# Merging the rows of one token over all four experts of a batch, so that both adding scatters write to the output itself

## The chip, the cores and the metric

The kernel runs on one core of a Trainium2 chip. The metric is the device time of one execution in microseconds (us), as the median over several runs; lower is better. The engines are named as in the profile: PE is TensorE's matmul and PEld its weight load, DVE is VectorE, ACT is ScalarE, POOL is GpSimd, SP is SyncE, which here only issues transfers.

## The reference, cut to what matters

Two layers work on x of shape (64, 64, 256), that is T = 4096 tokens of 256 numbers: an attention, a feed-forward over kept tokens, a second attention, and a mixture of experts. Only the last is touched by the change:

```python
logits = x @ gate_w.T                       # 64 experts
probs = softmax(logits); w, sel = top_k(probs, 8); w = w / sum(w)
# each expert takes its first CAP = 64 tokens; a token has up to 8 experts
h = silu(inp @ wg[e]) * (inp @ wu[e])       # (64, 96) per expert
out = h @ wd[e]                             # (64, 256) per expert
y = zeros((T, 256)).at[tok].add(g)          # g: out's rows times w
x = x + y
```

So each of 64 experts yields 64 rows, and each row is added to the row of its token. One token can occur in several experts, thus up to 8 rows are added to the same row of the output.

## The kernel before, in words

The first stages (two attentions, feed-forward, routing) keep the tokens in SBUF, write the residual to the DRAM array `out`, and write the normalised rows with their expert shares to the DRAM array `table`. `fill_slots` (lines 1254 to 1321) finds for each of the 4096 expert slots the token that sits in it; `k.token` is a 128 x 32 array of token numbers, one column for a *pair* of experts (64 slots each, 128 partitions). An empty slot gets the number T + partition, a spare row behind the tokens (L1296 to L1300). `k.move` (L1303) is the distance from a slot's token to its spare row.

`experts` (lines 1325 to 1502) works in 16 batches of four experts, that is two pairs, p = 0 and 1. Each engine has its own instruction stream, and semaphores couple them. For batch n:

- POOL gathers the 2 x 128 rows from `table` with two indirect transfers (L1361), five batches ahead of use. In the loop it first issues the two adding scatters of batch n (L1378), then the two gathers of batch n + 5. There are none left to issue from batch 11 on.
- PE turns the gathered rows (L1400), spreads the token numbers over a row (L1406), which waits until DVE has made the twins of the batch before (L1404), multiplies by the down weights of batch n - 1 (L1415) and by the gate and up weights of batch n (L1426), merges batch n - 1 (L1435) and turns the hidden values (L1442).
- ACT copies the turned rows (L1452), takes the silu (L1456), copies the merged sums of batch n - 1 into `add` (L1463) and then the turned hidden values (L1468). `add` has two places, so L1463 of batch m waits until both scatters of batch m - 2 have landed (L1461, L1462). ACT works in order: what stands behind that wait waits too, and so do PE and DVE.
- DVE copies the down result (L1478), makes the hidden values (L1486), and for each pair a 128 x 128 *twin* matrix that is 1 where two slots hold the same token (L1494). L1494 also counts these per row. L1497 to L1501 then send the second copy of a token to its spare row instead.
- SP loads the weights of batch n + 9 as soon as batch n has used its own (ring of 9 places, seven such loads of 768 + 384 KB in this stage).

The merge and the redirection hold within one pair alone: twin times part gives each slot the sum over both slots of the pair that have its token. Between the two pairs of a batch the same token can still occur, and two adding transfers in flight must not touch the same row. So pair 0 is added to `out` and pair 1 to a second array `extra`, which SP has filled with zeros long before (L1584, L1586), and each scatter waits only for the scatter of the batch before to its own array:

```python
for p, sum_of, landed in ((0, out, e_added), (1, extra, e_extra)):
    if n:
        pool.wait_ge(landed, 16 * n)
    pool.indirect_dma_start(out=sum_of[:, :], ..., compute_op=ALU.add).then_inc(landed, 16)
```

At the end POOL waits for the last scatters, and four transfers of 1 MB each add `extra` to `out` (L1387, the "joining transfers"). After them the program only clears semaphores and passes a barrier.

Of the kernel before, what the change touches and what calls it, by code (L numbers as in the profile page):

```python
# [12 lines left out]
P = 128  # L13
B, S, D = 64, 64, 256
C = 128
T = B * S
# [1237 lines left out]
def fill_slots(nc, ins, k, bank, stack):  # L1254
# [29 lines left out]
    def vector(dve):  # L1284
        dve.wait_ge(k.r_found, NT // GT)
        first_of(dve, k.found[:, :], best, s_max, s_rep)
        dve.wait_ge(s_backc, 1)
        first_of(dve, both[:, :], first[:, 0, :], s_max2, s_rep2)
        dve.wait_ge(s_max2, rounds)
        dve.tensor_copy(first[:, 1, :], first[:, 0, :]).then_inc(s_dup, 1)  # L1290
        dve.wait_ge(s_last, 1)
        for h in range(2):
            rows = slice(64 * h, 64 * h + 64)
            dve.tensor_copy(value[rows, :], bank(2)[rows, 0:E].rearrange("p (j e) -> p j e", e=2)[:, :, h]).then_inc(s_value_s, 1)
        dve.wait_ge(s_value_s, 2)
        dve.tensor_scalar(empty[:, :], value[:, :], 0.0, k.row_number[:, 0:1], ALU.is_equal, ALU.mult).then_inc(s_empty_s, 1)  # L1296
# [6 lines left out]
        dve.tensor_scalar(k.move[:, :], k.token[:, :], -1.0, k.spare_row[:, 0:1], ALU.mult, ALU.add).then_inc(s_move, 1)  # L1303
        dve.wait_ge(s_move, 1)
# [20 lines left out]
def experts(nc, ins, k, bank, out, extra, table):  # L1325

    with ExitStack() as stack:
# [5 lines left out]
        twin = z.sb("e_twin", [P, 2, 2, P])  # L1333
        count, again = z.sb("e_count", [P, 2, 2]), z.sb("e_again", [P, 2, 2])
# [6 lines left out]
        (e_idx_s, e_got0, e_got1, e_got2, e_got3, e_got4, e_got5, e_gotT, e_gotTc, e_row, e_twin_s, e_again_s, e_shift_s, e_to_s,  # L1341
         e_gu, e_silu, e_hid_s, e_hidT, e_hidTc, e_y, e_part_s, e_sum, e_add_s, e_added, e_extra, e_joined
         ) = z.sems(
             "e_idx_s e_got0 e_got1 e_got2 e_got3 e_got4 e_got5 e_gotT e_gotTc e_row e_twin_s e_again_s e_shift_s e_to_s "
             "e_gu e_silu e_hid_s e_hidT e_hidTc e_y e_part_s e_sum e_add_s e_added e_extra e_joined")
# [10 lines left out]
        def gpsimd(pool):  # L1356
            def gather(n, p):
                if n >= GOT_E:
                    pool.wait_ge(e_gotT, n - GOT_E + 1)
                    pool.wait_ge(e_hid_s, 4 * (n - GOT_E + 1))  # L1360
                pool.indirect_dma_start(out=got[:, n % GOT_E, p, :], out_offset=None, in_=table[:, :],  # L1361
                                        in_offset=bass.IndirectOffsetOnAxis(ap=idx[:, 2 * n + p:2 * n + p + 1], axis=0)
                                        ).then_inc(got_in[n % GOT_E], 16)

            pool.wait_ge(k.rows_set, 32 * (NT // GT))
            pool.wait_ge(k.pads, 16 * (3 + NT // 4))
            pool.wait_ge(k.out_set, 16 * NT)
            pool.wait_ge(e_idx_s, 1)
            for n in range(GOT_E - 1):
                for p in range(2):  # L1370
                    gather(n, p)
            for n in range(NB_E):
                pool.wait_ge(e_to_s, n + 1)
                pool.wait_ge(e_add_s, n + 1)
                for p, sum_of, landed in ((0, out, e_added), (1, extra, e_extra)):
                    if n:
                        pool.wait_ge(landed, 16 * n)
                    pool.indirect_dma_start(out=sum_of[:, :], out_offset=bass.IndirectOffsetOnAxis(ap=to[:, n, p:p + 1], axis=0),  # L1378
                                            in_=add[:, n % 2, p, :], in_offset=None, compute_op=ALU.add).then_inc(landed, 16)
                for p in range(2):  # L1380
                    if n + GOT_E - 1 < NB_E:
                        gather(n + GOT_E - 1, p)
            pool.wait_ge(e_added, 16 * NB_E)
            pool.wait_ge(e_extra, 16 * NB_E)
            for c in range(4):
                rows = slice(c * T // 4, (c + 1) * T // 4)
                pool.dma_start(out=out[rows, :].rearrange("(a b) d -> a (b d)", b=4), in_=extra[rows, :].rearrange("(a b) d -> a (b d)", b=4),  # L1387
                               accum_op=ALU.add, max_dma_last_dim=8192).then_inc(e_joined, 16)
            pool.wait_ge(e_joined, 64)

        def tensor(pe):
            for n in range(NB_E + 1):
                v, w, m = n % 2, (n - 1) % 2, n - 1
                if n < NB_E:
# [8 lines left out]
                    if n:  # L1403
                        pe.wait_ge(e_twin_s, 2 * n)  # L1404
# [24 lines left out]
                if n:  # L1429
                    pe.wait_ge(e_part_s, n)  # L1430
                    pe.wait_ge(e_twin_s, 2 * n)
# [13 lines left out]
        def scalar(act):  # L1445
            for n in range(NB_E + 1):
# [23 lines left out]
        def vector(dve):  # L1470
            dve.tensor_copy(idx[:, :], k.token[:, :]).then_inc(e_idx_s, 1)  # L1471
            for n in range(NB_E + 1):
# [6 lines left out]
                if n < NB_E:  # L1479
# [31 lines left out]
def program(nc, ins, out, extra, table):  # L1511
    with ExitStack() as stack:
# [22 lines left out]
        k.row_number, k.spare_row, k.second = z.sb("row_number", [P, 1]), z.sb("spare_row", [P, 1]), z.sb("second", [P, 1])  # L1535
# [207 lines left out]
        x = experts(nc, ins, k, bank, out, extra, table)  # L1743
# [27 lines left out]
def shape_constants():  # L1771
# [12 lines left out]
        "row_number": p[:, None].astype(np.float32),  # L1784
        "spare_row": (T + p)[:, None].astype(np.float32),
# [57 lines left out]
```

## Time and profile before

| what | value |
|---|---|
| median of 3 runs | 1038.46 us (1035.84 to 1041.59) |
| the profiled execution, its own time | 1038.37 us |
| its span in the profile | 1036.6 us |
| mean granted clock of TensorE | 0.938 |
| PE busy in the span | 853.5 us (82%) |
| DVE / ACT / POOL busy | 663.1 / 425.1 / 338.0 us |
| the stage with the experts | from about 888 us to the end |

The span counts from the first to the last instruction of the profiled execution; its own time is 1.8 us longer and lies within 0.1 us of the median. A row of a timeline is: start, duration, engine, line, operation, output from input, and in brackets how long the engine had stood idle before it and what ended that. The time of an indirect transfer on POOL is the time in which POOL writes its descriptors, not that in which data moves; its landing is seen by what waits for it. A row of busy times by stretches gives, for a stretch, its length, the busy time of PE, PEld, DVE, ACT and POOL with their counts, the granted clock of PE, the mean busy share of the 16 DMA engines, and GB/s.

### The profile page before, as it was taken

The numbers are of one execution on the slowest core, as the hardware profiler recorded it, in microseconds if no ns is written. First come the engines' busy times: TensorE is split into PE (matmuls) and PEld (weight loads), VectorE is DVE, ScalarE is ACT, GpSimd is POOL, SyncE is SP. The second block draws the span as 40 slices with busy tenths as digits, with TensorE's granted clock in tenths as the row PEclk, the third lists the DMA queues.
The fourth block names the chain that finished last, engine by engine and source line by source line (L and its number), as shares of the span: only waits on it lengthen the run. The fifth ranks groups of instructions, "written<-read, shape, count | busy, mean of one in ns | idle before, by whom it ended". The sixth has DMA issues, their size and how long they took to land. (4 is left out here: it accounts for less than half of the span.)

```text
span 1036.6 us, 25512 instructions
## 1 busy us (share of the span) xinstructions
PE 853.5 (82%) x9176; PEld 659.7 (64%) x9176; DVE 663.1 (64%) x1469; ACT 425.1 (41%) x1011; POOL 338.0 (33%) x297
## 2 busy tenths in 40 slices
PE   1799999999999899999889999999998830468730
PEld 0577777777777689899667777777776720245520
DVE  5577777777777665555367777777775589344520
ACT  1243443444444433334365555566656730123210
POOL 1443343443433040000133333333332010367860
PEclk9899999999999999999999999999999875698985
DMA  9300000000005000000011111111110494397557
GB/s 297 84 14 14 15 10 15 15 10 15 15 10 185 4 12 0 0 0 0 3 18 25 30 30 30 30 30 30 30 33 22 139 347 133 93 272 180 92 62 151
DMA packets 79561, 64.78 MB, mean 62 GB/s; under 512 B 41120, under 2 KB 74144, under 8 KB 79008
## 3 DMA queue, kind: packets, MB, share of 16 engines
q1 hardware_dynamic: 72800, 50.62, 16.7%
q0 software_dynamic: 6720, 13.64, 7.1%
q8 instruction: 24, 0.39, 0.2%
q14 instruction: 17, 0.14, 0.0%
HBM read 45.97 MB, written 22.45 MB: 66 GB/s over the span
## 5 line engine op out<-in xcount | busy, mean ns | idle before, releaser
L402 ACT ACTIVATE pr_t<-bank 128x512 f32<-128x512 f32 x128 | 76.4, 597 | 160.8 <-PE bank L298 160.0
L822 POOL TENSOR_TENSOR g_k_bd<-g_k_t,head_mask 128x1024 f32<-128x1024 f32 x32 | 60.6, 1893 | 134.8 <-ACT g_k_t L997 134.8
L310 PEld LDWEIGHTS bank<-v_bd,pr_t 128*64 128x64 f32 x2048 | 70.0, 137 | 26.6 <-issue 26.4
L298 PE MATMUL bank<-ident,sub 128*128 128x128 f32 x512 | 82.5, 284 | 3.6 <-ACT pr_t L402 2.8
L310 PE MATMUL bank<-v_bd,pr_t 128*64 128x18 f32 x2048 | 82.8, 214 | 0.1
L298 PEld LDWEIGHTS bank<-ident,sub 128*128 128x128 f32 x512 | 56.1, 141 | 31.4 <-issue 17.6
L479 DVE TENSOR_TENSOR sub<-bank,top 128x2048 f32<-128x2048 f32 x32 | 73.3, 2292 | 3.9
L259 POOL TENSOR_TENSOR rot<-part_a,part_b 128x512 f32<-128x512 f32 x32 | 40.7, 1273 | 103.8 <-DVE part_b L488 103.8
L475 DVE TENSOR_REDUCE top<-bank 128x32 f32<-128x2048 f32 x32 | 73.1, 2285 | 0.6 <-PE bank L286 0.4
L817 POOL TENSOR_TENSOR xres<-xres,g_out_bias 128x256 f32 (+1 forms) x32 | 23.3, 728 | 152.5 <-DVE g_xn L1020 152.5
L646 ACT ACTIVATE f_hid<-bank,b 128x128 f32<-128x128 f32 x128 | 36.5, 368 | 85.6 <-PE bank L592 85.6
L267 POOL TENSOR_TENSOR k_bd<-qk_t,head_mask 128x1024 f32<-128x1024 f32 x32 | 60.6, 1893 | 31.2 <-ACT qk_t L417 31.2
L592 PE MATMUL bank<-f_xs_t,w 128*128 128x128 f32 x512 | 63.8, 278 | 0.0
L592 PEld LDWEIGHTS bank<-f_xs_t,w 128*128 128x128 f32 x512 | 59.6, 192 | 5.0 <-ACT f_hid L646 4.6
L630 PE MATMUL bank<-w,f_hid 128*128 128x256 f32 x256 | 57.9, 379 | 0.0
L954 ACT ACTIVATE g_sq<-g_qk 128x512 f32<-128x512 f32 x32 | 20.2, 630 | 81.8 <-DVE g_qk L1070 81.8
L630 PEld LDWEIGHTS bank<-w,f_hid 128*128 128x128 f32 x256 | 47.4, 190 | 5.8
L1361 POOL DMA_INDIRECT e_got<-table,e_idx x32 | 31.8, 994 | 55.9 <-DVE e_idx L1471 46.4
L488 DVE TENSOR_TENSOR part_a<-bank,cos_t 128x512 f32<-128x512 f32 x32 | 22.2, 692 | 38.2 <-PE bank L359 38.2
L262 POOL TENSOR_TENSOR xres<-xres,bo 128x256 f32 (+1 forms) x32 | 23.3, 729 | 69.9 <-DVE xn L470 69.9
L875 PEld LDWEIGHTS bank<-g_v_bd,g_pr_t 128*64 128x64 f32 x1024 | 35.3, 136 | 15.7 <-issue 15.7
L964 ACT ACTIVATE g_pr_t<-bank 128x512 f32<-128x512 f32 x64 | 38.2, 597 | 16.7 <-PE bank L861 15.9
(196 smaller groups left out, 2008.8 us busy)
## 6 DMA issues: line engine op xcount, KB each, us to landing
e_w_gu<-in_experts_in SPq DMA_DIRECT2D x16, 768.0 KB, 14.0
e_w_d<-in_experts_out SPq DMA_DIRECT2D x16, 384.0 KB, 17.0
table<-r_row SPq DMA_DIRECT2D x16, 320.0 KB, 8.4
xres<-in_x SPq DMA_DIRECT2D x4, 1024.0 KB, 9.4
extra<-zero SPq DMA_DIRECT2D x8, 512.0 KB, 5.8
out<-xres SPq DMA_DIRECT2D x32, 128.0 KB, 1.7
out<-extra POOLq DMA_DIRECT2D x4, 1024.0 KB, 14.1
keys_in<-in_ctx_t SPq DMA_DIRECT2D x32, 64.0 KB, 1.8
```

Of the source, the lines that this page charges most:

```text
L259: pool.tensor_tensor(rot[:, v, :], part_a[:, v, :], part_b[:, v, :], ALU.add).then_inc(a_rot, 1)
L267: pool.tensor_tensor(k_bd[:, v, :, :, :, :].rearrange("p c b h s -> p (c b) h s"), qk_t[:, v, KC:2 * KC, :].rearrange("p c (b a s) -> p (c ...
L298: m = pe.transpose(b_pr[:, j * P:(j + 1) * P], sub[:, v, cols], k.ident[:, :])
L310: m = pe.matmul(b_o[64 * b:64 * b + 64, hp * VW0:(hp + 1) * VW0], pr_t[:, e, j, b * S:(b + 1) * S], v_bd[:, v, b, hp, :], start=True, stop ...
L402: act.activation(pr_t[:, e, :, :].rearrange("p j q -> p (j q)"), b_pr[:, :], ACT.Exp).then_inc(a_exp, 1)
L475: dve.tensor_reduce(top[:, :], sc, AX.X, ALU.max).then_inc(a_top, 1)
L479: dve.tensor_tensor(sub[:, u, :].rearrange("p (h s) -> p h s", s=S), sc, stretch(top[:, :], S), ALU.subtract).then_inc(a_sub, 1)
L592: mm = pe.matmul(b_h[half][:, (c % 4) * P:(c % 4 + 1) * P], k.w1[:, d, c * P:(c + 1) * P], xs_t[:, u, d, :], start=(d == 0), stop=(d == KC ...
L630: mm = pe.matmul(b_y[:, 0:D], hid[:, u, c, :], k.w2[:, c, :], start=(c == 0), stop=(c == FC - 1))
L646: act.activation(hid[:, u, c, :], b_h[c // 4][:, (c % 4) * P:(c % 4 + 1) * P], ACT.Gelu_apprx_tanh, bias=k.b1[:, c:c + 1]).then_inc(f_gelu, 1)
L822: pool.tensor_tensor(k_bd[:, v, :, :, :, :].rearrange("p c b h s -> p (c b) h s"), k_t[:, v, :, :].rearrange("p c (b a s) -> p (c b) a s", ...
L964: act.activation(pr_t[:, e, :, :].rearrange("p j q -> p (j q)"), b_pr[:, :], ACT.Exp).then_inc(g_exp, 1)
```

## The change

The twins are now made between all four experts of a batch: two pairs times two pairs, four 128 x 128 matrices instead of two. The merging matmul sums over both pairs, so each slot gets the sum over the whole batch. The first occurrence in the batch keeps its token's row, every other goes to a spare row; with two pairs there are 2 x 128 spare rows. All rows that the two scatters of a batch touch then differ, and both go to `out`. Both scatters of a batch wait until both of the batch before have landed. `extra`, its zero fill and the joining transfers are gone.

```diff
-            pool.wait_ge(k.pads, 16 * (3 + NT // 4))
+            pool.wait_ge(k.pads, 16 * 4)
...
-                for p, sum_of, landed in ((0, out, e_added), (1, extra, e_extra)):
-                    if n:
-                        pool.wait_ge(landed, 16 * n)
-                    pool.indirect_dma_start(out=sum_of[:, :], out_offset=bass.IndirectOffsetOnAxis(ap=to[:, n, p:p + 1], axis=0),
-                                            in_=add[:, n % 2, p, :], in_offset=None, compute_op=ALU.add).then_inc(landed, 16)
+                if n:
+                    pool.wait_ge(e_added, 32 * n)
+                for p in range(2):
+                    pool.indirect_dma_start(out=out[:, :], out_offset=bass.IndirectOffsetOnAxis(ap=to[:, n, p:p + 1], axis=0),
+                                            in_=add[:, n % 2, p, :], in_offset=None, compute_op=ALU.add).then_inc(e_added, 16)
...
-            pool.wait_ge(e_added, 16 * NB_E)
-            pool.wait_ge(e_extra, 16 * NB_E)
-            for c in range(4):
-                rows = slice(c * T // 4, (c + 1) * T // 4)
-                pool.dma_start(out=out[rows, :].rearrange("(a b) d -> a (b d)", b=4), in_=extra[rows, :].rearrange("(a b) d -> a (b d)", b=4),
-                               accum_op=ALU.add, max_dma_last_dim=8192).then_inc(e_joined, 16)
-            pool.wait_ge(e_joined, 64)
+            pool.wait_ge(e_added, 32 * NB_E)
...
                     if n:
-                        pe.wait_ge(e_twin_s, 2 * n)
+                        pe.wait_ge(e_twin_s, 4 * n)
...
                     for p in range(2):
-                        mm = pe.matmul(b_sum[:, p * D:(p + 1) * D], twin[:, w, p, :], part[:, w, p, :], start=True, stop=True)
+                        for q in range(2):
+                            mm = pe.matmul(b_sum[:, p * D:(p + 1) * D], twin[:, w, q, p, :], part[:, w, q, :],
+                                           start=(q == 0), stop=(q == 1))
...
                     if n >= 3:
-                        act.wait_ge(e_added, 16 * (n - 2))
-                        act.wait_ge(e_extra, 16 * (n - 2))
+                        act.wait_ge(e_added, 32 * (n - 2))
...
+                    for q in range(2):
+                        for p in range(2):
+                            dve.tensor_scalar(twin[:, v, q, p, :], b_row[:, p * P:(p + 1) * P], k.token[:, 2 * n + q:2 * n + q + 1],
+                                              None, ALU.is_equal, ALU.add, accum_out=count[:, v, q, p:p + 1]).then_inc(e_twin_s, 1)
+                    dve.wait_ge(e_twin_s, 4 * (n + 1))
                     for p in range(2):
-                        dve.tensor_scalar(twin[:, v, p, :], b_row[:, p * P:(p + 1) * P], k.token[:, 2 * n + p:2 * n + p + 1],
-                                          None, ALU.is_equal, ALU.add, accum_out=count[:, v, p:p + 1]).then_inc(e_twin_s, 1)
-                    dve.wait_ge(e_twin_s, 2 * (n + 1))
-                    dve.tensor_scalar(again[:, v, :], count[:, v, :], -1.0, k.second[:, 0:1], ALU.add, ALU.mult).then_inc(e_again_s, 1)
-                    dve.wait_ge(e_again_s, n + 1)
+                        dve.tensor_scalar(front[:, v, p:p + 1], count[:, v, p, p:p + 1], -1.0, k.second[:, 0:1],
+                                          ALU.add, ALU.mult).then_inc(e_front_s, 1)
+                    dve.wait_ge(e_front_s, 2 * (n + 1))
+                    dve.tensor_copy(again[:, v, 0:1], front[:, v, 0:1]).then_inc(e_again_s, 1)
+                    dve.tensor_scalar(again[:, v, 1:2], front[:, v, 1:2], count[:, v, 1, 0:1], 0.5, ALU.add, ALU.is_gt).then_inc(e_again_s, 1)
+                    dve.wait_ge(e_again_s, 2 * (n + 1))
...
-            sp.dma_start(out[T:T + P, :], k.zero[:, 0:D]).then_inc(k.pads, 16)
-            sp.dma_start(table[T:T + P, :], k.zero[:, :]).then_inc(k.pads, 16)
-            for c in range(NT // 4):
-                sp.dma_start(extra[4 * P * c:4 * P * (c + 1), :].rearrange("(t p) d -> p t d", p=P),
-                             spread(k.zero[:, 0:D], 4)).then_inc(k.pads, 16)
-            sp.dma_start(extra[T:T + P, :], k.zero[:, 0:D]).then_inc(k.pads, 16)
+            for h in range(2):
+                sp.dma_start(out[T + h * P:T + (h + 1) * P, :], k.zero[:, 0:D]).then_inc(k.pads, 16)
+                sp.dma_start(table[T + h * P:T + (h + 1) * P, :], k.zero[:, :]).then_inc(k.pads, 16)
```

In `fill_slots` the constants `row_number` and `spare_row` become 128 x 32 arrays, with 128 more in the columns of pair 1, and L1296 and L1303 become `scalar_tensor_tensor` with them as second input.

## Rows read from the trace of the kernel before

**Rows 1.** The chain of waits, 996 to 1037 us: start, duration, what.
```profile
996.61 3.75 DMA out<-e_add,e_to
...
1003.00 3.80 DMA extra<-e_add,e_to
```

**Rows 2.** The joining transfers' line L1387: issue and landing.
```profile
L1387 POOL DMA_DIRECT2D out<-extra x4: 934/1307/1766, 1007.4 to 1009.1; - x4
...
DMA to landing us min/median/max: 7.6/14.1/20.6
```

**Rows 3.** Busy time by stretches, the end of the span.
```profile
1010.00:1028.00 18.00, 0.00 (x0) 0.00 (x0) 0.00 (x0) 0.00 (x0) 0.86 (x2) 0.50 1.04 215
```

**Rows 4.** Timeline of POOL, batches without gathers.
```profile
987.43 1.55 POOL L1378 DMA_INDIRECT out<-e_add,e_to  x1 [1.25 <-DMA out<-e_add,e_to]
989.28 1.55 POOL L1378 DMA_INDIRECT extra<-e_add,e_to  x1 [0.30 <-issue]
...
1001.14 1.55 POOL L1378 DMA_INDIRECT out<-e_add,e_to  x1 [1.12 <-DMA out<-e_add,e_to]
```

**Rows 5.** Timeline of POOL, a batch with gathers after the weight loads.
```profile
957.03 1.61 POOL L1378 DMA_INDIRECT out<-e_add,e_to  x1 [0.30 <-issue]
958.95 1.57 POOL L1378 DMA_INDIRECT extra<-e_add,e_to  x1 [0.30 <-issue]
...
963.44 1.62 POOL L1378 DMA_INDIRECT out<-e_add,e_to  x1 [0.30 <-DVE e_to L1501]
...
982.69 1.61 POOL L1378 DMA_INDIRECT out<-e_add,e_to  x1 [0.30 <-issue]
```

**Rows 6.** Timeline of POOL, batches beside the weight loads.
```profile
907.01 1.64 POOL L1378 DMA_INDIRECT out<-e_add,e_to  x1 [5.05 <-DVE e_to L1501]
...
914.21 1.62 POOL L1378 DMA_INDIRECT out<-e_add,e_to  x1 [1.06 <-issue]
...
922.16 1.62 POOL L1378 DMA_INDIRECT out<-e_add,e_to  x1 [1.84 <-DMA out<-e_add,e_to]
...
932.85 1.58 POOL L1378 DMA_INDIRECT extra<-e_add,e_to  x1 [2.66 <-DMA extra<-e_add,e_to]
...
943.78 1.61 POOL L1378 DMA_INDIRECT out<-e_add,e_to  x1 [0.30 <-issue]
```

**Rows 7.** Timeline of ACT: copies into add that waited for a landing.
```profile
922.13 0.60 ACT L1463 ACTIVATE e_add<-bank 128x512 f32<-128x512 f32 x1 [2.26 <-DMA extra<-e_add,e_to]
...
950.49 0.60 ACT L1463 ACTIVATE e_add<-bank 128x512 f32<-128x512 f32 x1 [0.55 <-DMA extra<-e_add,e_to]
...
962.87 0.60 ACT L1463 ACTIVATE e_add<-bank 128x512 f32<-128x512 f32 x1 [2.47 <-DMA extra<-e_add,e_to]
```

**Rows 8.** Busy time by stretches, with and without weight loads.
```profile
904.00:950.00 46.00, 35.26 (x256) 24.07 (x256) 22.71 (x86) 12.77 (x29) 31.21 (x24) 0.89 0.93 254
952.00:980.00 28.00, 23.03 (x176) 15.81 (x175) 13.86 (x53) 8.27 (x19) 22.59 (x18) 0.94 0.56 90
```

**Rows 9.** Timeline, all engines: an unblocked batch, and the clock's low stretch.
```profile
954.72 1.13 PE L1435 MATMUL bank<-e_part,e_twin 128*128 128x256 f32 x4
954.84 0.33 ACT L1456 ACTIVATE e_act_g<-bank 128x192 f32<-128x192 f32 x1 [1.97 <-PE bank L1426]
...
956.58 0.35 DVE L1494 TENSOR_SCALAR_CACHE_REDUCE e_twin<-bank,token 128x128 f32<-128x128 f32 x1
...
956.61 0.42 PE L1442 MATMUL bank<-ident,e_hid 128*96 128x128 f32 x2 [0.75 <-DVE e_hid L1486]
...
957.13 0.09 DVE L1494 DVE_READ_ACCUMULATOR e_twin<-bank,token 128x1 f32 x1
...
960.07 0.33 ACT L1456 ACTIVATE e_act_g<-bank 128x192 f32<-128x192 f32 x1 [1.97 <-PE bank L1426]
...
974.29 0.33 ACT L1456 ACTIVATE e_act_g<-bank 128x192 f32<-128x192 f32 x1 [3.68 <-PE bank L1426]
```

**Rows 10.** Transfers issued by SP: the zero fill of extra.
```profile
323.19 9.03 SPq L1584 DMA_DIRECT2D extra<-zero  x8
```

More of the change, by code:

```diff
@@ L1295, in vector @@
         dve.wait_ge(s_value_s, 2)
-        dve.tensor_scalar(empty[:, :], value[:, :], 0.0, k.row_number[:, 0:1], ALU.is_equal, ALU.mult).then_inc(s_empty_s, 1)
+        dve.scalar_tensor_tensor(out=empty[:, :], in0=value[:, :], scalar=0.0, in1=k.row_number[:, :],
+                                 op0=ALU.is_equal, op1=ALU.mult).then_inc(s_empty_s, 1)
         dve.tensor_scalar(name[:, :], value[:, :], -1.0, float(T), ALU.mult, ALU.add).then_inc(s_name_s, 1)
@@ L1301, in vector @@
         dve.wait_ge(s_token, 1)
-        dve.tensor_scalar(k.move[:, :], k.token[:, :], -1.0, k.spare_row[:, 0:1], ALU.mult, ALU.add).then_inc(s_move, 1)
+        dve.scalar_tensor_tensor(out=k.move[:, :], in0=k.token[:, :], scalar=-1.0, in1=k.spare_row[:, :],
+                                 op0=ALU.mult, op1=ALU.add).then_inc(s_move, 1)
         dve.wait_ge(s_move, 1)
@@ L1321, in fill_slots, with experts @@
     return Stage(z.signals, sync=sync, tensor=tensor, scalar=scalar, vector=vector)
-def experts(nc, ins, k, bank, out, extra, table):
+def experts(nc, ins, k, bank, out, table):
     with ExitStack() as stack:
@@ L1332, in experts @@
         got_t = z.sb("e_got_t", [P, 2, 2, KC, P])
-        twin = z.sb("e_twin", [P, 2, 2, P])
-        count, again = z.sb("e_count", [P, 2, 2]), z.sb("e_again", [P, 2, 2])
+        twin = z.sb("e_twin", [P, 2, 2, 2, P])
+        count, front = z.sb("e_count", [P, 2, 2, 2]), z.sb("e_front", [P, 2, 2])
+        again = z.sb("e_again", [P, 2, 2])
         shift = z.sb("e_shift", [P, 2, 2])
@@ L1340, in experts @@
         add = z.sb("e_add", [P, 2, 2, D])
-        (e_idx_s, e_got0, e_got1, e_got2, e_got3, e_got4, e_got5, e_gotT, e_gotTc, e_row, e_twin_s, e_again_s, e_shift_s, e_to_s,
-         e_gu, e_silu, e_hid_s, e_hidT, e_hidTc, e_y, e_part_s, e_sum, e_add_s, e_added, e_extra, e_joined
+        (e_idx_s, e_got0, e_got1, e_got2, e_got3, e_got4, e_got5, e_gotT, e_gotTc, e_row, e_twin_s, e_front_s, e_again_s, e_shift_s, e_to_s,
+         e_gu, e_silu, e_hid_s, e_hidT, e_hidTc, e_y, e_part_s, e_sum, e_add_s, e_added
          ) = z.sems(
-             "e_idx_s e_got0 e_got1 e_got2 e_got3 e_got4 e_got5 e_gotT e_gotTc e_row e_twin_s e_again_s e_shift_s e_to_s "
-             "e_gu e_silu e_hid_s e_hidT e_hidTc e_y e_part_s e_sum e_add_s e_added e_extra e_joined")
+             "e_idx_s e_got0 e_got1 e_got2 e_got3 e_got4 e_got5 e_gotT e_gotTc e_row e_twin_s e_front_s e_again_s e_shift_s e_to_s "
+             "e_gu e_silu e_hid_s e_hidT e_hidTc e_y e_part_s e_sum e_add_s e_added")
         got_in = [e_got0, e_got1, e_got2, e_got3, e_got4, e_got5]
@@ L1430, in tensor @@
                     pe.wait_ge(e_part_s, n)
-                    pe.wait_ge(e_twin_s, 2 * n)
+                    pe.wait_ge(e_twin_s, 4 * n)
                     if n >= 2:
@@ L1508, in over_rows, with program @@
     return vector.rearrange("(a d) -> a d", a=1).to_broadcast([rows, vector.shape[0]])
-def program(nc, ins, out, extra, table):
+def program(nc, ins, out, table):
     with ExitStack() as stack:
@@ L1534, in program @@
         k.countdown = z.sb("countdown", [P, NT])
-        k.row_number, k.spare_row, k.second = z.sb("row_number", [P, 1]), z.sb("spare_row", [P, 1]), z.sb("second", [P, 1])
+        k.row_number, k.spare_row, k.second = z.sb("row_number", [P, NP_E]), z.sb("spare_row", [P, NP_E]), z.sb("second", [P, 1])
         k.token, k.move, k.idx = z.sb("token", [P, NP_E]), z.sb("move", [P, NP_E]), z.sb("e_idx", [P, NP_E], U32)
@@ L1741, in program @@
         nc.all_engine_barrier()
-        x = experts(nc, ins, k, bank, out, extra, table)
+        x = experts(nc, ins, k, bank, out, table)
         inner = stack.enter_context(ExitStack())
@@ L1783, in shape_constants @@
         "countdown": (T - P * np.arange(NT).reshape(2, NT // 2).T.reshape(1, NT) - p[:, None]).astype(np.float32),
-        "row_number": p[:, None].astype(np.float32),
-        "spare_row": (T + p)[:, None].astype(np.float32),
+        "row_number": (p[:, None] + P * (np.arange(NP_E) % 2)).astype(np.float32),
+        "spare_row": (T + p[:, None] + P * (np.arange(NP_E) % 2)).astype(np.float32),
         "second": (p >= CAP)[:, None].astype(np.float32),
@@ L1835 @@
            for n, v in laid.items()}
-    out = nc.dram_tensor("out", [T + P, D], F32, kind="ExternalOutput").ap()
-    extra = nc.dram_tensor("extra", [T + P, D], F32, kind="Internal").ap()
-    table = nc.dram_tensor("table", [T + P, ROW], F32, kind="Internal").ap()
-    program(nc, ins, out, extra, table)
+    out = nc.dram_tensor("out", [T + 2 * P, D], F32, kind="ExternalOutput").ap()
+    table = nc.dram_tensor("table", [T + 2 * P, ROW], F32, kind="Internal").ap()
+    program(nc, ins, out, table)
     r = run_bass_kernel_spmd(nc, [arrays], core_ids=[0])
```

## The prediction

> **What bounds the kernel now.** I read the chain of waits at the end of the span first, because the change removes the last thing in it. The last scatter to `extra` starts at 1003.00 us and lands 3.80 us later, at 1006.80; only then does POOL issue the four joining transfers [rows 1]. They are issued from 1007.4 to 1009.1, and the longest landing takes 20.6 us, so the last one lands at 1029.7 [rows 2]. For 18 us of that the 16 DMA engines are full (share 1.04) at 215 GB/s, and every compute engine stands still [rows 3]. That is 22.9 us, from 1006.8 to 1029.7, with nothing beside them.
>
> Then I read POOL's timeline in the stage of the experts, to see what sets the pace of the 16 batches. There are three regimes, and the reader should see that the change meets each differently.
>
> - Batches 11 to 15 have no gathers left. A first scatter starts 4.6 us after the one before, when that one has landed: from 982.69 to 1001.14, four periods take 18.45 us [rows 4, 5].
> - Batches 7 to 10 are full of POOL's own work: two scatters and two gathers follow each other with gaps of 0.30 us, and the period is 6.41 us (957.03 to 963.44) [rows 5].
> - Batches 0 to 6 run while SP's seven weight loads fill the DMA engines: share 0.93 against 0.56 later [rows 8]. Landings are late, and the seven periods from 907.01 to 957.03 take 50.0 us, 7.15 each [rows 5, 6].
>
> PE, DVE and ACT are not the limit there. Where nothing blocks them a batch takes 5.23 us, from the silu at 954.84 to that at 960.07 [rows 9], and they wait at the copy into `add` for scatters to land [rows 7].
>
> **The change part by part.** The sum is made against the profiled execution, 1038.4 us, which is the median of the runs shown within 0.1 us.
>
> *Joining transfers gone: -22.9 us.* Worked out above. Behind the last landing the program ends as before. The last batch needs both scatters landed, which it needed before too.
>
> The Trainium skill, "DMA: Bandwidth & Descriptors", section "Anatomy of one DMA — SWDGE (gpsimd) path", fits a transfer issued by GpSimd as 2.0 us plus bytes over 436 GB/s. By it 4.2 MB would be an estimated 11.6 us, half of what the rows show, and the change would lose about 2 us instead of gaining. The trace does not agree: 18 us and more of full DMA engines, presumably because an adding transfer also reads what it adds to. The rows leave that course no chance, and the sum goes by them.
>
> *Tail, four periods: +7.3 us.* A first scatter now waits for both scatters of the batch before. The second starts 1.85 us after the first (987.43 and 989.28 [rows 4]), lands 3.80 later [rows 1], and POOL starts 0.78 after a landing it waited for (a scatter of 996.61 lands 3.75 later, at 1000.36, and the next starts at 1001.14 [rows 1, 4]). A period is 1.85 + 3.80 + 0.78 = 6.43, and 6.50 where gathers still made the first longer (1.61 in place of 1.55). Together 25.8 against 18.45.
>
> *Batches 7 to 10: +0.4 us.* Here the wait is nearly hidden by the two gathers: the second scatter starts at 1.92, lands at 5.72, POOL is ready to start at 6.50, against 6.41 now. So 4 x 0.1. If the lag is part of the 0.30 gap, nothing.
>
> *Batches 0 to 6: +4.4 us, the term that I know least.* In the present landings a period would be: batch 1, second landing just before 922.13, so 922.0 - 914.21 + 0.78 = 8.6 (ACT starts 0.1 behind a landing, as 962.87 is against 958.95 + 3.80); batch 2, 932.85 - 922.16 = 10.7; batch 5, 950.4 - 943.78 + 0.78 = 7.4 [rows 5 to 7]. With 8.6 for batch 0, 7.4 for 3 and 4 as for 5, and 6.5 for batch 6, the seven give 56.6, that is +6.6. The lower bound is 0: the loads' bytes are fixed, and with more time between them landings come sooner; the wait only adds, so I exclude a gain. Between them I go by the DMA share. At 0.93 the loss would be 6.6, at 0.56 it is 7 x 0.1 = 0.7. The 46 us at 0.93 are 42.8 us of full DMA engines; spread over 50 us that is a share of 0.86, over 54 us 0.79 [rows 8]. I take 0.79, an estimate, since the loads follow compute, which now waits too, and interpolate: 0.7 + 5.9 x 0.23/0.37 = 4.4 (at 0.86 it would be 5.5).
>
> The same page, section "Latency and other measured facts", says that HBM access takes longer under load and the fixed cost of a transfer is smaller with less. If that were all, the loss would sit near 0.7 and the sum near 1025.4.
>
> *More twins, more merging: +1.5 us once, else hidden.* DVE makes two more twins per batch. Two take 0.64 from the first's start to the last read of its count (956.58 to 957.22), so two more are 0.6. PE's L1406 of the next batch waits for them, and behind it stand L1415 and L1426 of PE and then silu: the unblocked batch becomes 5.8. PE merges with eight passes in place of four, +1.0 (four take 1.13); it waited 0.75 before L1442 anyway, so this stays under the twins [rows 9]. DVE's small steps (two fronts, a copy and a compare in place of one operation) cost at most as much again as two twins, 0.6, an estimate, and end before the copy of the down result is due; the scatter's indices are a batch ahead. 5.8 is below 6.4, so POOL covers all this; without that cover it is 0.6 per batch. Only batch 0 has none: its scatter waits for twins (+0.6) and merge (+0.95), so it starts 1.5 late. Bounds 0.6 to 2.
>
> *At nothing:* the zero fill and its nine issues (8 take 9.03 us of SP [rows 10]; no engine waited for them, and SP's next loads came later); the larger constants and pads, for the same reason; two DVE operations of 128 x 32 with another form, at most 0.1.
>
> **The sum.** -22.9 + 7.3 + 0.4 + 4.4 + 1.5 = -9.3: **1029.1 us**. The range of this case: 1024.7 (nothing lost in batches 0 to 6) to 1031.8 (6.6 lost, batch 0 late by 2).
>
> **The rivals.**
>
> *Contention feeds itself, 1036 us.* With both scatters due before either of the next, a late landing stops POOL, then ACT at `add`, then PE, DVE and the loads behind them, which then bunch. If five of the seven periods took 9.65, the mean of those worked out for batches 1 and 2, and two 6.5, they make 61.3, a loss of 11.3 in place of 4.4: 1036.0. For it: share 0.93, and batch 2 [rows 6, 8]. Against: the loads are only seven, and slower compute spaces them.
>
> *Compute becomes the bound, 1037 us.* The granted clock has a mean of 0.94 from 952 to 980, which is 3.4 us at the lower of its two levels, 1.2 GHz [rows 8]. The silu of 974.29 waited 3.68 for PE in place of 1.97: +1.7 [rows 9]. An unblocked batch at that level is 5.8 + 1.7, and 1.0 more for the longer merge, 8.5 against POOL's 6.5. If four more batches fell there, 4 x 2.0 = 8. For it: PE's waits become longer. Against: PE also gets more work, and `add` is one batch ahead.
>
> *Two adding scatters into one array hinder each other: slower, up to 1065 us.* No row shows this; before, the two in flight had different arrays. Place: the landing of each second scatter. Price: of 3.80 us, 2.25 lie behind the 1.55 in which POOL writes descriptors; served one after the other, 16 x 2.25 = 36 [rows 1, 4]. From 0.6 us per batch on the gain is gone (9.3/16), from 0.9 on it is slower than can be told from no change. Against: the rows that they touch differ.
>
> *The joining was worth less than it shows* (it does not do what it says): only if something else held the end; after 1006.8 nothing else runs [rows 3]. I give it nothing.
>
> **How the numbers follow.** A measurement of this kernel can tell about 0.5%, 5.2 us, from no change. Forecast 0.66; nothing lost beside the loads, at the low end near 1024.7, 0.10; contention 0.12; compute 0.06; hindering scatters 0.06. The first two are faster by over 5.2 us almost always, contention half of the time: 0.82. Within: the other half, compute, and a part of the forecast's edge: 0.12. Slower: 0.06. The range 1024.5 to 1034.0 takes in the forecast's bounds and the nearer half of contention.
>
> **What would show it.** No DMA-bound stretch at the end, and about 7 us from the last landing to the end. First scatters 6.4 to 6.5 apart from batch 7 to 15, now alike with and without gathers. Batch 0's first scatter at 908.5, batch 7's near 962.9, batch 15's near 1014.7 in place of 1001.14, which is also 908.5 + 54.4 + 4 x 6.5 + 25.8. Wrong would be: a second scatter landing later than 3.8 us after its start where no loads run (the third rival), ACT's silu periods above 6.5 with PE at the lower clock (the second), batch 7 behind 966 (the first).

## The result and the profile after

The changed kernel takes 1035.05 us (median of 20 runs), against 1038.43 for the kernel before (also 20); the ratio is 0.9964, with a 95% interval of 0.9947 to 0.9982. It is faster by 3.7 us (1.9 to 5.5), which is within the 0.5% that the prediction called no change. The forecast was 1029.1 us, 9.3 less, with a range of 1024.5 to 1034.0; the measured time lies above that range. The profiled execution took 1035.25 us with a span of 1033.4.

The joining transfers are gone, but most of their 22.9 us has come back as waits between scatters. POOL's timeline of the changed kernel shows where (start, duration, operation, idle time before it):

```profile
889.70 1.21 POOL L1364 DMA_INDIRECT e_got<-table,e_idx  x1 [46.34 <-DVE e_idx L1469]
...
909.59 1.63 POOL L1381 DMA_INDIRECT out<-e_add,e_to  x1 [7.40 <-ACT e_add L1461]
...
918.53 1.62 POOL L1381 DMA_INDIRECT out<-e_add,e_to  x1 [2.82 <-DMA out<-e_add,e_to]
...
926.12 1.62 POOL L1381 DMA_INDIRECT out<-e_add,e_to  x1 [1.48 <-ACT e_add L1461]
...
937.25 1.62 POOL L1381 DMA_INDIRECT out<-e_add,e_to  x1 [5.02 <-ACT e_add L1461]
939.17 1.58 POOL L1381 DMA_INDIRECT out<-e_add,e_to  x1 [0.30 <-issue]
...
946.91 1.62 POOL L1381 DMA_INDIRECT out<-e_add,e_to  x1 [3.55 <-ACT e_add L1461]
...
956.08 1.62 POOL L1381 DMA_INDIRECT out<-e_add,e_to  x1 [3.06 <-ACT e_add L1461]
...
969.29 1.62 POOL L1381 DMA_INDIRECT out<-e_add,e_to  x1 [0.50 <-ACT e_add L1461]
...
995.40 1.62 POOL L1381 DMA_INDIRECT out<-e_add,e_to  x1 [0.41 <-issue]
...
1021.29 1.56 POOL L1381 DMA_INDIRECT out<-e_add,e_to  x1 [2.90 <-DMA out<-e_add,e_to]
1023.15 1.56 POOL L1381 DMA_INDIRECT out<-e_add,e_to  x1 [0.30 <-issue]
```

Read the first scatters of the batches against [rows 4 to 6]. Batch 0 starts at 909.59, batch 7 at 969.29, batch 11 at 995.40, batch 15 at 1021.29. Batch 7 behind 966 was the prediction's sign for its rival "contention feeds itself". From these the whole difference of the spans (3.2 us) can be laid out:

| stretch, us | before | after | difference | forecast |
|---|---|---|---|---|
| start to first gather | 889.45 | 889.70 | +0.3 | 0 |
| first gather to batch 0 | 17.56 | 19.89 | +2.3 | +1.5 |
| batches 0 to 7, seven periods | 50.02 | 59.70 | **+9.7** | **+4.4** |
| batches 7 to 11 | 25.66 | 26.11 | +0.4 | +0.4 |
| batches 11 to 15 | 18.45 | 25.89 | +7.4 | +7.3 |
| batch 15 to the end | 35.46 | 12.11 | -23.3 | -22.9 |

Five of the six are within 1 us of the forecast. The miss is the stretch beside the weight loads, where the seven periods are 8.94, 7.59, 11.13, 9.66, 9.17, 6.58 and 6.63 us (batches 0 to 6).

The chain of waits of the changed kernel (start, duration, what) shows what the periods of batches 2 and 3 are made of:

```profile
928.05 8.38 DMA out<-e_add,e_to
936.43 0.02 issue
936.45 0.02 ACTq L1460
936.47 0.04 issue
936.51 0.61 ACT e_add L1461
937.12 0.13 issue
937.25 0.30 POOL out L1381
...
939.17 6.92 DMA out<-e_add,e_to
```

The second scatter of batch 2 starts at 928.05 and lands 8.38 us later, at 936.43. That one landing releases two engines: ACT, whose copy for batch 4 starts at 936.51, and POOL, whose scatter of batch 3 starts at 937.25. (The release of POOL is put down to ACT's copy, though POOL's scatter is of batch 3, whose copy ended at 926.05; 937.25 is 0.82 after the landing, the usual lag behind a landing.) ACT's release lets PE go on, and PE's matmuls let SP load the next weights. SP's timeline:

```profile
939.49 0.33 SPq L1247 DMA_DIRECT2D e_w_gu<-in_experts_in  x1
939.86 0.43 SPq L1249 DMA_DIRECT2D e_w_d<-in_experts_out  x1
```

So a load of 1.2 MB (768 + 384 KB) is issued 0.3 us after the batch's second scatter, which then lands 6.92 us after its start. PE's clock has a part in this moment: the granted clock had fallen to 0.50 behind PE's wait for ACT, and L1412 took 1.98 us for eight passes instead of 1.08. What that shift by 0.9 us is worth was not tried.

Not every load follows a landing, however. The first five of the seven loads come at PE's own pace; the second to fifth are 5.8 us apart. The last two, at 939.49 above and at 948.26, come later because of the waits:

```profile
910.74 0.33 SPq L1247 DMA_DIRECT2D e_w_gu<-in_experts_in  x1
...
916.52 0.33 SPq L1247 DMA_DIRECT2D e_w_gu<-in_experts_in  x1
...
922.28 0.33 SPq L1247 DMA_DIRECT2D e_w_gu<-in_experts_in  x1
...
928.16 0.33 SPq L1247 DMA_DIRECT2D e_w_gu<-in_experts_in  x1
...
948.26 0.33 SPq L1247 DMA_DIRECT2D e_w_gu<-in_experts_in  x1
```

The load of 928.16 starts 0.1 us after the second scatter of batch 2, the one that took 8.38 us to land. The kernel before has the same meeting, and nearly the same landing (timeline of POOL, then of SP):

```profile
924.08 1.57 POOL L1378 DMA_INDIRECT extra<-e_add,e_to  x1 [0.30 <-issue]
...
924.22 0.33 SPq L1247 DMA_DIRECT2D e_w_gu<-in_experts_in  x1
```

That scatter landed about 8.0 us after its start, since the next one to `extra` began at 932.85 [rows 6], which by the usual lag is 0.78 behind the landing. But the first scatter of the next batch, to `out`, did not wait for it and had begun at 928.57, 6.41 after the one before. With the common wait the period is 11.13. So in batches 0 to 2 landings that were about as late before now cost their full length, and in batches 3 and 4 the loads come, in addition, 2 to 3 us behind the landing that was waited for, that is beside the next second scatter (939.49 and 948.26; second scatters at 939.17 and 948.84).

The busy times by stretches (length, PE, PEld, DVE, ACT, POOL, granted clock, DMA share, GB/s) show, around batch 3, the DMA engines doing almost nothing while everything waits, and then everything at once:

```profile
936.00:938.00 2.00, 0.57 (x4) 0.38 (x6) 0.00 (x0) 1.35 (x3) 0.75 (x1) 0.67 0.05 18
938.00:940.00 2.00, 2.00 (x14) 1.26 (x12) 0.55 (x1) 0.00 (x0) 1.70 (x2) 0.50 0.35 34
940.00:942.00 2.00, 2.00 (x15) 1.12 (x11) 0.15 (x1) 0.00 (x0) 1.70 (x2) 0.50 0.94 172
942.00:944.00 2.00, 2.00 (x6) 1.68 (x7) 1.49 (x5) 0.33 (x1) 1.06 (x2) 0.62 0.95 376
```

### The profile page after: what moved, and what is told of

It reads as the page before. It is cut to its first block and busy times, and to the rows that moved or that the text cites. A ratio compares the mean times of both kernels' runs of the same rounds, so it can differ in the third digit from the quotient of the medians.

```text
span 1033.4 us, 25740 instructions
## 1 busy us (share of the span) xinstructions
PE 870.1 (84%) x9240; PEld 673.2 (65%) x9240; DVE 676.8 (65%) x1581; ACT 424.2 (41%) x1011; POOL 335.0 (32%) x293
## 5 line engine op out<-in xcount | busy, mean ns | idle before, releaser
L310 PEld LDWEIGHTS bank<-v_bd,pr_t 128*64 128x64 f32 x2048 | 70.0, 137 | 26.5 <-issue 26.3
L1381 POOL DMA_INDIRECT out<-e_add,e_to x32 | 50.9, 1590 | 42.9 <-ACT e_add L1461 27.1
L592 PE MATMUL bank<-f_xs_t,w 128*128 128x128 f32 x512 | 63.8, 278 | 0.0
```

Source lines behind the costliest of these rows:

```text
L310: m = pe.matmul(b_o[64 * b:64 * b + 64, hp * VW0:(hp + 1) * VW0], pr_t[:, e, j, b * S:(b + 1) * S], v_bd[:, v, b, hp, :], start=True, stop ...
L592: mm = pe.matmul(b_h[half][:, (c % 4) * P:(c % 4 + 1) * P], k.w1[:, d, c * P:(c + 1) * P], xs_t[:, u, d, :], start=(d == 0), stop=(d == KC ...
L1381: pool.indirect_dma_start(out=out[:, :], out_offset=bass.IndirectOffsetOnAxis(ap=to[:, n, p:p + 1], axis=0), in_=add[:, n % 2, p, :], in_o ...
```

## The experiments

Three theories stood against each other. *Theory 1*: the common wait (no scatter of a batch before both of the last have landed) releases scatters and load in step, and turns every late landing into lost time. These are two claims, and the runs below bear on them differently. *Theory 2*: two adding scatters into one array hinder each other. *Theory 3*: the larger merge slows compute. Profiles of different runs differ by up to 5 us in when the experts' stage begins (first gather from 884.5 to 889.7), so the runs are compared by their periods inside the stage, in us, and by their ratios of times. Ratios are against the kernel before; the reference times of before in these rounds were 1037.0 to 1037.4 us.

| run | median | ratio (95%) | batches 0-7 | 7-11 | 11-15 |
|---|---|---|---|---|---|
| before | 1038.4 | 1 | 50.0 | 25.7 | 18.5 |
| changed | 1035.1 | 0.9964 (0.9947 to 0.9982) | 59.7 | 26.1 | 25.9 |
| no_join | 1012.3 | 0.9762 (0.9723 to 0.9801) | 50.0 | 25.7 | 18.3 |
| pair_wait | 1061.2 | 1.0237 (1.0198 to 1.0276) | 63.8 | 26.2 | 26.3 |
| merge_alone | 1038.8 | 1.0014 (0.9993 to 1.0035) | 50.2 | 25.7 | 18.3 |
| after_no_loads | 1019.6 | 0.9835 (0.9805 to 0.9866) | 46.8 | 26.7 | 25.8 |
| before_no_loads | 1032.5 | 0.9955 (0.9929 to 0.9981) | 45.0 | 25.7 | 18.4 |
| small_runs | 1033.2 | 0.9972 (0.9948 to 0.9997) | 60.4 | 26.3 | 25.9 |
| whole_late | 1028.8 | 0.9909 (0.9869 to 0.9949) | 55.0 | 26.7 | 25.8 |
| thirds_at_once | 1034.9 | 0.9972 (0.9957 to 0.9987) | 57.8 | 26.6 | 25.9 |
| paced_thirds | 1026.0 | 0.9899 (0.9869 to 0.9930) | 47.8 | 26.5 | 28.4 |
| paced_early | 1022.9 | 0.9866 (0.9845 to 0.9886) | 48.4 | 27.0 | 25.5 |
| before_paced | 1033.9 | 0.9965 (0.9949 to 0.9981) | 46.5 | 27.1 | 18.8 |

### The change taken apart: no_join, pair_wait, merge_alone

**no_join.** The kernel before without the joining transfers; half of the sums are missing from its output.

```diff
-            for c in range(4):
-                rows = slice(c * T // 4, (c + 1) * T // 4)
-                pool.dma_start(out=out[rows, :]..., in_=extra[rows, :]..., accum_op=ALU.add, ...).then_inc(e_joined, 16)
-            pool.wait_ge(e_joined, 64)
```

> The kernel before without the four joining transfers; the half of the sums in extra is left out of the output. Both theories (what was lost lies beside the weight loads; or the scatters into one array hinder each other) say the same here: the joining was worth 22.9 us, so the time is about 1015.5 us, and the batches keep their starts (seven periods of 7.15 us, then 6.4, then 4.6).

Measured: 1012.3 us. By the ratio the joining cost 24.7 us (20.6 to 28.7), in agreement with the 22.9 of the trace. The time is 3 us below the 1015.5 expected; the profile's stage of experts starts 3.6 us earlier than before (first gather at 885.88). The largest term of the sum was right.

**pair_wait.** The kernel before, with the common wait alone; arrays, merge and joining stay.

```diff
+                if n:
+                    pool.wait_ge(e_added, 16 * n)
+                    pool.wait_ge(e_extra, 16 * n)
                 for p, sum_of, landed in ((0, out, e_added), (1, extra, e_extra)):
-                    if n:
-                        pool.wait_ge(landed, 16 * n)
```

> The kernel before with one edit: both scatters of a batch wait for both of the batch before; two arrays, the small merge and the joining transfers stay. Theory 1 (the common wait lets weight loads and scatters start together, so that landings stay late): the seven first periods go from 50.0 to 57 to 60 us, the tail's four from 18.4 to 25.9, and the time is 1053 to 1056 us. Theory 2 (two adding scatters into one array hinder each other): here they have two arrays, so the first seven periods take at most 53 us and landings beside the loads are as before; the time is 1046 to 1049 us. Theory 3 (the larger merge slows compute, and that costs the time): as theory 2.

Measured: 1061.2 us, +24.6 us by the ratio (20.5 to 28.6). The wait alone costs what the joining gives. It is above what theory 1 had said (1053 to 1056), and far from theories 2 and 3. Here the scatters go to two arrays and the merge is small, and still the first seven periods take 63.8 us. Its second scatters beside the loads land 6.6 to 8.2 us after their start. The same alternation of empty and full DMA engines stands in its busy times by stretches:

```profile
936.00:938.00 2.00, 1.82 (x10) 1.07 (x12) 0.00 (x0) 0.61 (x2) 1.69 (x2) 0.50 0.03 8
938.00:940.00 2.00, 2.00 (x16) 1.50 (x14) 0.69 (x1) 0.00 (x0) 1.70 (x2) 0.50 1.01 119
...
942.00:944.00 2.00, 1.30 (x9) 0.82 (x8) 1.62 (x9) 0.00 (x0) 0.10 (x1) 1.00 1.04 279
...
946.00:948.00 2.00, 1.77 (x20) 1.38 (x22) 0.64 (x1) 0.67 (x2) 1.66 (x2) 1.00 0.00 0
```

**merge_alone.** The changed kernel given back its two arrays, own waits, zero fill and joining, so that only the merge over four experts is new.

```diff
-                if n:
-                    pool.wait_ge(e_added, 32 * n)
-                for p in range(2):
-                    pool.indirect_dma_start(out=out[:, :], ...).then_inc(e_added, 16)
+                for p, sum_of, landed in ((0, out, e_added), (1, extra, e_extra)):
+                    if n:
+                        pool.wait_ge(landed, 16 * n)
+                    pool.indirect_dma_start(out=sum_of[:, :], ...).then_inc(landed, 16)
...
+            (the four joining transfers and the zero fill of extra, as before)
```

> The changed kernel with two arrays, each scatter waiting for its own array alone, zero fill and joining transfers: against the kernel before only the merge over four experts is new. Theory 1: batch 0 starts 2.3 us late and the seven first periods stay near 50 us, so 1040 to 1042 us. Theory 3 (compute): the seven first periods take 55 us or more, so over 1045 us. Theory 2 says as theory 1.

Measured: 1038.8 us, +1.5 by the ratio, with an interval that includes no change, and a little below the 1040 to 1042 that theory 1 had said. From the first scatter on it keeps the pace of before; the stage begins with the first gather at 885.64:

```profile
905.61 1.64 POOL L1381 DMA_INDIRECT out<-e_add,e_to  x1 [7.45 <-ACT e_add L1468]
...
955.76 1.61 POOL L1381 DMA_INDIRECT out<-e_add,e_to  x1 [0.30 <-issue]
```

The seven periods take 50.15 us; from first gather to batch 0 it is 19.97, as in the changed kernel. Theory 3 falls, and the late start of batch 0 belongs to the merge. The other profiles agree: from first gather to batch 0 the five with the small merge take 16.3 to 18.5 us, the eight with the large one 19.5 to 21.0, by the means 3.1 more.

### The loads: after_no_loads, before_no_loads

Both leave out the seven loads, so batches 9 to 15 multiply by the weights of batches 0 to 6:

```diff
-            for n in range(RING_E, NB_E):
-                sp.wait_ge(e_gu, n - RING_E + 1)
-                sp.wait_ge(e_y, n - RING_E + 1)
-                load_experts(sp, ins, k, n)
...
-                    pe.wait_ge(k.w_in[n % RING_E], 32 * (n // RING_E + 1))
+                    pe.wait_ge(k.w_in[n % RING_E], 32)
```

> The changed kernel without the seven weight loads beside the experts; batches 9 to 15 multiply by the weights of batches 0 to 6, so their output is not the reference's. Theory 1: with no loads each of the first seven periods is 6.4 to 6.6 us, 45.5 in all in place of 59.7, and the time is about 1021 us (14 less than 1035). Theory 2: landings stay late at 8 us or more after the first scatter, the seven take over 55 us, and the time is over 1030 us. Theory 3: between, with ACT's silu periods and not landings setting the pace.

Measured: 1019.6 us, 17.1 less than before by the ratio and so about 13.4 less than the changed kernel. The seven periods fall from 59.7 to 46.8, six of them at 6.5 to 6.6:

```profile
905.46 1.63 POOL L1378 DMA_INDIRECT out<-e_add,e_to  x1 [8.49 <-DVE e_to L1502]
...
952.25 1.62 POOL L1378 DMA_INDIRECT out<-e_add,e_to  x1 [0.47 <-DVE e_to L1502]
```

With both scatters in one array and no loads beside them, the periods are those of a landing in quiet. Theory 2 falls here too.

> The kernel before without the seven weight loads beside the experts (batches 9 to 15 multiply by the weights of batches 0 to 6, so that their output is not the reference's). Theory 1 (the common wait turns what the loads delay into lost time, and two arrays hide most of it): the seven first periods go from 50.0 to 45 us, so 1032 to 1033 us, a third of the 15.4 us that the changed kernel gained by the same edit. If the loads cost both kernels alike, it gains 15 us too, 1022 us, and the common wait is not what makes them dear.

Measured: 1032.5 us, 4.7 less (2.0 to 7.4). The same seven loads cost the kernel before 5 us and the changed one over 13. The loads are the same; the common wait makes them dear. That late landings become lost time is shown by these two runs and pair_wait.

### When and how the loads are issued

**small_runs** was to tell whether the length of the loads' runs matters.

```diff
-                load_experts(sp, ins, k, n)
+                sp.dma_start(k.w_gu[:, n % RING_E, :, :, :].rearrange("p e c i -> p (e c) i"), ...)
+                sp.dma_start(k.w_d[:, n % RING_E, :, :], ...)
```

> The changed kernel with the same loads at the same moments, written as runs of 1536 and 1024 bytes instead of 6144 and 4096. If a scatter's rows of 1 KB are held up because each waits behind one long run of the loads, shorter runs let them land earlier: seven periods of 52 to 56 us in place of 59.7, and 1027 to 1032 us. If it is the loads' bytes alone, or if the shorter runs take longer for the same bytes, the seven take 59 us or more, and 1035 us or more.

Inconclusive: its page counts the same packets as the changed kernel's, so the transfers had stayed the same and the question stays open. As a repeat of the changed kernel it gives the spread: 60.4 against 59.7 us for the seven periods. The line of its page on DMA packets:

```profile
DMA packets 74906, 56.61 MB, mean 55 GB/s; under 512 B 40944, under 2 KB 70000, under 8 KB 74864
```

**whole_late** has the whole loads wait for a landing too, the one that also releases the next first scatter:

```diff
                 sp.wait_ge(e_y, n - RING_E + 1)
+                sp.wait_ge(e_added, 32 * (n - RING_E + 1))
                 load_experts(sp, ins, k, n)
```

> The changed kernel with the whole loads, each released in addition by the landing of the batch's own scatters, that is up to 5 us later or at the moment at which the next scatter is issued. Theory 1, as far as the moment counts: a load of 1.1 MB still takes over 3 us of full engines and reaches into the scatters' data, so the seven periods take 54 to 60 us, and the time is 1030 to 1036 us. If the moment were all, they would take below 52 us, and 1027 us or less.

Measured: 1028.8 us, with 55.0 us for the seven periods, now at 6.6 to 9.6 instead of up to 11.1. The time is below the 1030 to 1036 us expected. Moving the same transfers by some microseconds gives 4.7 us of the periods back; the moment counts, but is not all. It also corrects theory 1: here every load is released by the same landing as a scatter, and yet less is lost. Such a load is issued about 0.7 us ahead of the first scatter of a batch, as in batch 2 (timeline of SP, then of POOL):

```profile
922.96 0.33 SPq L1247 DMA_DIRECT2D e_w_gu<-in_experts_in  x1
...
923.69 1.62 POOL L1382 DMA_INDIRECT out<-e_add,e_to  x1 [3.47 <-ACT e_add L1462]
```

In the changed kernel the loads beside the three longest periods come within 0.6 us of the second scatter. So what hurts is not the shared release itself, but at what moment of the period the load comes, and how much of it.

**thirds_at_once** and **paced_thirds** cut each load in three pieces of 384 KB (two of the gate and up weights, one of the down weights). The first issues all three as the whole load is issued now. The second releases two at each landing up to batch 8, then one. In both, PE waits for all three pieces of a batch before it multiplies by its gate and up weights (80 in place of 64 arrivals; the diffs below leave that line out).

```diff
-                load_experts(sp, ins, k, n)
+                for part in range(3):
+                    load_third(sp, ins, k, n, part)
```

> The changed kernel with each load cut into thirds, all three issued at the moments at which the whole load is issued now. Theory 1 (a load in one piece beside a scatter holds it up, and the thirds help only through their spacing): as the changed kernel, seven first periods of 57 to 61 us and 1033 to 1036 us. If the cutting itself did it, the seven take below 52 us and the time is about 1026 us.

```diff
+            pieces = [(n, part) for n in range(RING_E, NB_E) for part in range(3)]
+            for j in range(1, NB_E - 2):
+                sp.wait_ge(e_added, 32 * j)
+                for n, part in pieces[0:2 if j < 9 else 1]:
+                    sp.wait_ge(e_gu, n - RING_E + 1)
+                    sp.wait_ge(e_y, n - RING_E + 1)
+                    load_third(sp, ins, k, n, part)
+                pieces = pieces[2 if j < 9 else 1:]
```

> The changed kernel with the same loads in thirds of 384 KB, each released by the landing of the scatters of a batch: two at each of batches 1 to 8, one at each of 9 to 13. Theory 1: a third is through before the second scatter's data moves, and landings come near the 5.7 us of the unloaded batches; the first seven periods take 46 to 50 us, later ones stay below 6.8, and the time is 1021 to 1026 us. Rival (what counts is the bytes moved beside the scatters, whenever they are issued): the seven periods take 55 us or more and the time is 1031 to 1037 us.

Measured: cut but not spaced, 57.8 us for the seven and 1034.9 us, the changed kernel within the noise. Cut and spaced, 47.8 us and 1026.0 us. The bytes are the same in both, and cutting alone gives nothing clear; what does it is when the pieces are issued, that is spaced out and at a landing (the two together; whole_late shows the second to be a part of it). The late part of the forecast for paced_thirds failed in one place, the period before batch 14 took 9.02 us. Its timeline, all engines, says why:

```profile
994.50 0.33 SPq L1261 DMA_DIRECT2D e_w_d<-in_experts_out  x1
995.26 1.56 POOL L1398 DMA_INDIRECT out<-e_add,e_to  x1 [3.04 <-DMA out<-e_add,e_to]
...
998.07 2.83 PE L1440 MATMUL bank<-e_w_gu,e_got_t 128*64 128x192 f32 x16 [7.97 <-issue]
...
1004.28 1.56 POOL L1398 DMA_INDIRECT out<-e_add,e_to  x1 [5.59 <-ACT e_add L1478]
```

The last piece was issued at 994.50, and PE, which needs all three, stood 7.97 us, until 3.57 after that issue. **paced_early** issues two pieces at each landing until none is left:

```diff
-            for j in range(1, NB_E - 2):
+            for j in range(1, NB_E - 4):
...
-                for n, part in pieces[0:2 if j < 9 else 1]:
+                for n, part in pieces[0:2]:
```

> The paced thirds with two pieces at each landing until none is left (batches 1 to 11), so that the last piece is in two batches earlier. The period of 9.0 us before batch 14, in which PE waited for weights, should fall to 6.5; the first seven stay as they were. So 2.5 us less than the paced thirds: 1023 to 1024 us. If that period was not due to the last piece, no change.

Measured: 1022.9 us, the long period gone (6.16 us in place of 9.02), the best of all kernels here that leave nothing out: 1.3% faster than before and by the ratios about 10 us faster than the changed kernel. From 910 us to 974 its DMA share is above 0.5 in every stretch of 2 us:

```profile
936.00:938.00 2.00, 1.65 (x12) 0.95 (x13) 1.90 (x13) 1.35 (x3) 1.69 (x2) 1.00 0.78 183
938.00:940.00 2.00, 2.00 (x24) 1.51 (x24) 1.14 (x5) 0.00 (x0) 1.70 (x2) 1.00 1.07 207
940.00:942.00 2.00, 2.00 (x12) 1.44 (x8) 0.93 (x3) 0.33 (x1) 0.42 (x2) 1.00 0.54 150
```

**before_paced** is the kernel before with the same pacing (waits on e_added and e_extra at 16 * j).

> The kernel before with the same pacing of the loads (two thirds at each landing of both scatters). Theory 1: there the loads cost only the 4.8 us by which it is faster without them, so at most that is to be had: 1033 to 1037 us. If pacing gives as much as in the changed kernel (9 us), the loads' cost has nothing to do with the common wait: 1028 us.

Measured: 1033.9 us, 3.6 less than before (2.0 to 5.3), against 10 that the same pacing gave the changed kernel. This is what theory 1 says. Paced alike, the change is worth 10.3 us by the ratios (11.0 by the medians, 1033.9 and 1022.9), more than the 9.3 that were forecast for it.

## Why the prediction was wrong

**Joining transfers, -22.9: right.** 24.7 by no_join, 23.3 in the trace. The estimate from the Trainium skill ("DMA: Bandwidth & Descriptors", "Anatomy of one DMA — SWDGE (gpsimd) path"), 11.6 us for 4.2 MB, was rightly set aside: the trace does not agree with that fit for these adding transfers.

**Tail, +7.3: right** (+7.4). So was the period made of 1.85 + 3.80 + 0.78. **Batches 7 to 10, +0.4: right.**

**Batch 0 late by 1.5: too small**, above its upper bound of 2 too. It was 2.3 in the two profiles, 2.4 with the merge alone, 3.1 by the means of all profiles. In the changed kernel L1423 of batch 1 took 2.72 us for 16 passes, with PE's mean granted clock at 0.75 from 904 to 908; before, the engine was at the full clock at that point. Whether the merge delays the rise of the clock was not tried.

**Batches 0 to 6, +4.4: the step that failed.** It was +9.7, even above the upper bound of 6.6. The step interpolated by the mean DMA share: a stretch of 54 us has share 0.79, so landings must come sooner. The share did fall, to 0.75 over 904 to 960, lower than forecast, and landings did not come sooner: the second scatters of batches 2, 3 and 4 landed 8.38, 6.92 and 6.43 us after their start. A mean share says how much work there is, not whether it meets. From 914 to 936 the share was 0.99; from 936 to 958 it was 0.60, idle while POOL, ACT and SP all waited for one landing, and then full when that landing released a scatter and, through ACT and PE, a load. So the low share was made by the lost time and is no sign of relief. The interpolation accounts for 2.2 of the 5.3 us that are missing (from 6.6 down to 4.4).

The other 3.1 lie above the upper bound. That bound took the landings of the kernel before, and for batches 0 to 2 it was right: 27.9 us by it, 27.7 measured. For batches 3 and 4 it had 7.4 each, 14.8, and 18.8 were measured: there the waits had moved the loads to just beside the second scatter, which the bound could not see. Batches 5 and 6 took 0.7 less than it had. That the moved loads are what makes batches 3 and 4 long is read from the trace and fits whole_late; no run moved these two alone.

The Trainium skill ("DMA: Bandwidth & Descriptors", "Latency and other measured facts") says that less load on HBM means a smaller fixed cost of a transfer. The direction agrees with the run without loads, where most periods are 6.5 to 6.6 us. The loss near 0.7 that the prediction drew from it did not come, since the mean load says nothing of the load at the moment of a transfer.

**The rivals.** "Contention feeds itself" had the mechanism, a late landing stopping POOL, ACT, PE and the loads behind them, and its price: 1036 us against 1035.05, five long periods of 9.65 against five with a mean of 9.30. Its bunching of the loads came about only for the last two. It had a chance of 0.12, because "the loads are only seven, and slower compute spaces them": the loads are spaced, by 5.8 us, but at that spacing they kept the DMA engines at 0.99. The compute rival did not come about (merge_alone), nor did the hindering scatters (pair_wait, after_no_loads).

The parts alone, -24.7, +24.6 and +1.5, add up to +1.4, and the whole is -3.7. Within their intervals that need be no contradiction; it also fits that the changed kernel's seven periods are shorter than pair_wait's (59.7 and 63.8), perhaps since slower compute issues the early loads further apart (5.8 us, against 4.9 to 5.5 in pair_wait). That was not tried on its own.

## What to carry to other kernels

Before two waits are made one, look for landings in the trace that are late already and cost nothing, because only one of the two waits meets them: the common wait pays for each. Then list everything that the one landing will release, and follow each engine to the transfer that it issues next, to see at what moment of the period a load will come. A mean share of the DMA engines does not bound such a cost; the longest period of the trace, taken for every period beside the loads, did so here (10.7 us against a mean of 9.3 measured). And loads that are due nine batches later need not be issued as soon as their place is free: cut in pieces and issued at landings, they left the seven periods at 47.8 to 48.4 us, against 46.8 without any loads.

## What was not expected of the hardware

A scatter of 128 rows of 1 KB, which lands 3.8 us after its start in quiet, took 8.38 us beside one load of 1.2 MB and two gathers. The load itself is short: its two transfers land 4.6 to 4.9 and 5.3 to 5.8 us after their issue in this stage, and at the 376 GB/s of the fullest stretch above 1.2 MB would take 3.1 us, an estimate. A load issued at the landing, 2.7 us ahead of the second scatter, cost less (whole_late). The four joining transfers, 4.2 MB added from DRAM to DRAM, ran at 215 GB/s with the DMA engines full. Leaving them out saved 24.7 us (no_join). And the stages ahead of the experts vary from profile to profile: the changed kernel and the six edits of it that are the same up to there reach the first gather at 884.5 to 889.7 us, a spread of 5.2 us, more than the change is worth.
